# Keys and values of every fourth sequence of a cross attention projected during the feed-forward layer before it

## The reference

```python
x = x + _L0_ffn_ref(_layernorm(x, axis=-1), L0_ffn_w_gate, L0_ffn_w_up, L0_ffn_w_down)
x = x + _L1_xattn_ref(_layernorm(x, axis=-1), ctx_1024, ctx_1024, L1_xattn_Wq, ..., L1_xattn_bo)

def _L1_xattn_ref(x1, x2, Wq, bq, Wk, bk, Wv, bv, Wo, bo):
    q = x1 @ Wq.T + bq ; k = x2 @ Wk.T + bk ; v = x2 @ Wv.T + bv
    ...   # 16 heads
    attn = softmax(q k^T / 4) ; o = attn v
    return o @ Wo.T + bo
```

## Time and profile before

| | us |
|---|---|
| median of 3 runs | 1636.23 |
| lowest, highest | 1634.57, 1638.24 |
| the profiled execution: time | 1634.2 |
| its span | 1632.4 |

### The profile page before, as it was taken

One profiled execution on the slowest core, in us unless ns is written; L12 is line 12 of the kernel. 1 busy time (PEld: TensorE's weight loads), 2 busy tenths in 40 slices (PEclk: granted clock), 3 DMA queues, 4 the chain that ended last, 5 costly groups with the idle time before them and its releaser, 6 DMA issues.

```text
span 1632.4 us, 32837 instructions
## 1 busy us (share of the span) xinstructions
PE 1463.9 (90%) x12556; PEld 1127.3 (69%) x12556; DVE 897.7 (55%) x1896; ACT 712.2 (44%) x1761; POOL 498.9 (31%) x693
## 2 busy tenths in 40 slices
PE   3998996991799999999996688789999999999999
PEld 3887774431677777777775466548877885886787
DVE  3898897488545555565655588734224323422332
ACT  3887775395535554555553455421212211221221
POOL 1445551001026865865553577500000000000000
PEclk9999999995999999999998799989999999999999
DMA  7000000000031161145110000013321440342230
GB/s 280 24 10 2 1 0 1 1 0 27 14 130 40 39 237 46 39 142 211 39 32 2 1 2 0 1 45 136 135 104 50 153 159 13 136 163 76 91 136 13
DMA packets 49500, 111.38 MB, mean 68 GB/s; under 512 B 4240, under 2 KB 6800, under 8 KB 46864
## 3 DMA queue, kind: packets, MB, share of 16 engines
q1 hardware_dynamic: 49424, 110.36, 19.3%
HBM read 99.86 MB, written 10.49 MB: 68 GB/s over the span
## 4 chain that ended last, share of the span: by engine, by line
PE 70%; DVE 15%; issue 6%; POOL 5%; ACT 2%; DMA 1%; SPq 0%; DVEq 0%; POOLq 0%; ACTq 0%
PE ps L843 22%; PE ps L491 15%; PE ps L695 6%; PE ps L497 6%; PE ps L689 5%; PE ps L894 3%; PE ps L715 3%; DVE R L1223 2%; PE ps L667 2%; DVE R L1519 2%; PE ps L726 2%; DVE amax L1392 2%; POOL R L1792 1%; POOL R L1810 1%; PE ps L560 1%
## 5 line engine op out<-in xcount | busy, mean ns | idle before, releaser
L843 PE MATMUL ps<-R 128*128 128x256 f32 x1792 | 388.6, 379 | 3.4 <-DVE R L1649 3.4
L843 PEld LDWEIGHTS ps<-R 128*128 128x128 f32 x1792 | 340.0, 190 | 52.2 <-issue 6.5
L491 PE MATMUL ps<-R 128*128 128x128 f32 (+1 forms) x1344 | 307.3, 388 | 6.4 <-DVE R L1388 4.8
L491 PEld LDWEIGHTS ps<-R 128*128 128x128 f32 x1344 | 190.5, 194 | 119.3 <-issue 109.6
L1792 POOL TENSOR_TENSOR R<-R,c_inv 128x1024 f32<-128x1024 f32 x64 | 121.1, 1893 | 170.4 <-DVE c_inv L1558 170.4
L1109 ACT ACTIVATE R<-ps,c_nmx 128x257 f32<-128x257 f32 x256 | 118.0, 474 | 112.0 <-DVE c_nmx L1543 112.0
L1519 DVE COPY R<-ps 128x512 f32<-128x512 f32 x128 | 88.2, 689 | 106.3 <-PE ps L715 105.1
L689 PE MATMUL ps<-R,x_wk 128*128 128x256 f32 x512 | 128.6, 394 | 0.8 <-POOL R L1784 0.8
L695 PE MATMUL ps<-x_wv,R 128*128 128x256 f32 x512 | 121.1, 379 | 0.0
L1870 POOL TENSOR_SCALAR g_ve<-g_mv 128x4 f32<-128x4 f32 x4 | 0.9, 236 | 345.6 <-DVE g_mv L1611 345.6
L689 PEld LDWEIGHTS ps<-R,x_wk 128*128 128x128 f32 x512 | 92.7, 191 | 17.9 <-POOL R L1784 1.4
(11 more groups left out here) (205 smaller groups left out, 2463.4 us busy)
## 6 DMA issues: line engine op xcount, KB each, us to landing
R<-quadrant_sums SPq DMA_DIRECT2D x32, 1024.0 KB, 6.8
R<-in_f_hq SPq DMA_DIRECT2D x32, 768.0 KB, 4.6
R<-in_ctxT SPq DMA_DIRECT2D x64, 257.0 KB, 2.7
R<-in_f_hq SPq DMA_DIRECT2D x8, 1024.0 KB, 8.3
quadrant_sums<-R SPq DMA_DIRECT2D x8, 1024.0 KB, 7.6
R<-in_f_w SPq DMA_DIRECT2D x3, 1024.0 KB, 7.1
R<-in_ctxk SPq DMA_DIRECT2D x16, 128.0 KB, 2.1
out<-x SPq DMA_DIRECT2D x4, 512.0 KB, 2.6
```

The source lines that it names most:

```text
L491: r = mm(dst, w[:, ki, fo * P:(fo + 1) * P], src[:, ki, :], start=(ki == 0), stop=(ki == KI - 1))
L843: r = mm(ps[:, 4 * (g % 2) + bk, half * HALF:(half + 1) * HALF], f_wr[g % 3][:, w, ki * P:(ki + 1) * P], src[:, k, ki, :], start=(ki == 0) ...
```

## The change

Of each tile, the fourth sequence (u = 3) is projected earlier. Its 16 contexts ("ahead" 0 to 15) are loaded raw (without the last position) into three buffers; PE projects keys and values of them, where the subtraction of the last position is made otherwise: for keys it goes into the bias of ACT's copy (`kb_ahead`), for values a third matmul per half adds minus the last position's value to every row (`nvl_ahead`), so that `values_ahead` has six matmuls where `c_values` has four. ACT copies them out (`stage_ahead`) and SP stores them to a DRAM tensor `kv_ahead`. Ten of the sixteen lie on PE between the gate products and the down products; the other six lie between and behind the four down blocks (10, 11 and 12 behind the first three, 13 to 15 behind the last). In the loop the fourth sequence's keys and values are loaded back from `kv_ahead` (`load_keys`, `load_values`), so POOL's shift, PE's keys and values and ACT's copies are made for three of four sequences. `c_kT` has four buffers, one for each u.

The loop's steps are then: u = 0 as before (keys and values of this tile's third sequence). u = 1: scores, outputs, transposes of both halves of the probabilities, the second into bank 5 rather than 6, then keys of the next tile's first sequence, then `c_project_out`; no values. u = 2: scores, outputs, `c_turn`, first half of the values, transposes, second half of the values, transposes; no keys. u = 3: keys and values of the next tile's second sequence, in the old order. On DVE, at u = 1 the two copies come ahead of the extraction, and `c_add` and `last_stat` move behind the reciprocal. On POOL the shift ahead of step u = 0 is now that of the next tile's first sequence, for which SP can issue the transfer of tile 0 only when the last of the 16 stores has landed (the waits for `ahead_stored` stand in front of SP's loop). On ACT two, not three, up conversions precede the first gate conversion. Some semaphores are merged, and the small tile `w_int` lies in R.

```diff
+        AHEAD, AHEAD_PAUSE = T, 10
+
+        def ahead_no(j):
+            return j + 1 if j < AHEAD_PAUSE else j + 3
+
+        def ahead_bank(j):
+            return 2 * ((j + 1) % 4) if j < AHEAD_PAUSE else 4
+
+        def first_no(u):
+            return AHEAD_PAUSE + u + 1
+
+        def rest_no(m):
+            return AHEAD + m + 1
...
+            def load_ahead(j):
+
+                sp.dma_start(a_ctx[j % 3], A["ctxT"][SPT * j + 3, :, :, 0:S - 1]).then_inc(ctxk_in[j % 3], 16)
+
+            def store_ahead(j):
+
+                sp.wait_ge(k_copied, ahead_no(j))
+                sp.dma_start(kv_ahead[j, :, 0:2, :], a_kT[j % 3]).then_inc(ahead_stored[j % 3], 16)
+                sp.wait_ge(v_copied, ahead_no(j))
+                sp.dma_start(kv_ahead[j, :, 2:4, :].rearrange("p a b -> p (a b)"), a_v[j % 3])\
+                    .then_inc(ahead_stored[j % 3], 16)
...
+            def load_keys(i):
+
+                after(sp, c_s, 2 * SPT * i)
+                sp.dma_start(c_kT[3][:, :, 0:S - 1], kv_ahead[i, :, 0:2, :]).then_inc(k_loaded, 16)
+
+            def load_values(i):
+
+                after(sp, c_o, SPT * i)
+                sp.dma_start(c_v[3], kv_ahead[i, :, 2:4, :]).then_inc(v_loaded, 16)
...
+            for j in range(AHEAD):
+                if j + 3 < AHEAD:
+                    sp.wait_ge(v_ready, ahead_no(j))
+                    load_ahead(j + 3)
+                if j == 3:
+                    sp.wait_ge(f0_gj, 2)
+                    for n in range(3):
+                        sp.dma_start(c_ctx[n], A["ctxT"][n]).then_inc(ctx_in[n], 16)
+                if j >= 1:
+                    store_ahead(j - 1)
+                if j == 5:
+                    sp.wait_ge(ahead_stored[0], 32)
+                    load_keys(0)
+                    load_values(0)
+            store_ahead(AHEAD - 1)
+            for j in range(3):
+                sp.wait_ge(ahead_stored[j], 32 * ((AHEAD + 2 - j) // 3))
...
-                    sp.wait_ge(v_ready, n + 1)
-                    sp.dma_start(c_ctx[u], A["ctxT"][n + SPT]).then_inc(ctx_in[u], 16)
+                    if u < 3:
+                        sp.wait_ge(v_ready, rest_no(3 * i + u) if i or u == 2 else first_no(u))
+                        sp.dma_start(c_ctx[u], A["ctxT"][n + SPT]).then_inc(ctx_in[u], 16)
+                    if u == 1 and i:
+                        load_keys(i)
+                    if u == 3 and i:
+                        load_values(i)
...
-            def c_turn_probs(n, par, k):
-
-                after(pe, c_ptc, 2 * n + k)
+            def c_turn_probs(n, par, k, bank=6):
+
+                after(pe, c_ptc, 2 * n + (k if bank == 6 else 0))
                 for g in (2 * k, 2 * k + 1):
                     for c in range(2):
                         at = ((g % 2) * 2 + c) * P
-                        r = tr(ps[:, 6, at:at + P], c_p[par][:, g, c * P:(c + 1) * P], ident[:])
+                        r = tr(ps[:, bank, at:at + P], c_p[par][:, g, c * P:(c + 1) * P], ident[:])
                 r.then_inc(c_pt, 1)
...
-                pe.wait_ge(k_copied, n + 1)
+                if u == 3:
+                    pe.wait_ge(k_loaded, 16 * (i + 1))
+                else:
+                    pe.wait_ge(k_copied, rest_no(3 * i + u))
...
-                    c_outputs(n - 2, (u + 2) % SPT)
-                more = not (last and u >= 2)
+                    c_outputs(i if u >= 2 else i - 1, (u + 2) % SPT)
                 behind = not (first and u == 0)
-                if more:
-                    pe.wait_ge(ctx_shifted, n + 3)
-                    pe.wait_ge(k_copied, n + 2)
-                    c_keys((u + 2) % SPT)
-                after(pe, c_otc, n - 1)
-                if u == 1 and not first:
-                    c_project_out(i - 1)
-                if u == 2 and not last:
-                    c_turn(i + 1)
-                if u == 3 and not last:
-                    c_query(i + 1)
-                if behind:
-                    pe.wait_ge(c_nrm, n)
-                    c_turn_probs(n - 1, (u + 1) % 2, 0)
-                if more:
-                    pe.wait_ge(v_copied, n + 2)
+                done = 3 * i + 2 if u == 0 else 3 * i + 3 if u < 3 else 3 * i + 4
+
+                def keys():
+                    if u and last:
+                        return
+                    pe.wait_ge(ctx_shifted, done + 1)
+                    pe.wait_ge(k_copied, rest_no(done - 1))
+                    c_keys((2, 0, 0, 1)[u])
+
+                def probs(k, bank=6):
+                    if behind:
+                        pe.wait_ge(c_nrm, n)
+                        c_turn_probs(n - 1, (u + 1) % 2, k, bank)
+
+                def values(c):
+                    if u and last:
+                        return
+                    pe.wait_ge(v_copied, rest_no(done - 1))
+                    c_values((u + 2) % SPT, c)
+
+                if u == 1:
+                    probs(0)
+                    pe.wait_ge(v_copied, rest_no(3 * i + 2))
+                    probs(1, 5)
+                    keys()
+                    if not first:
+                        pe.wait_ge(c_otc, n - 1)
+                        c_project_out(i - 1)
+                elif u == 2:
+                    after(pe, c_otc, n - 1)
+                    if not last:
+                        c_turn(i + 1)
+                    values(0)
+                    probs(0)
+                    values(1)
+                    probs(1)
...
+            def keys_ahead(j, k):
+                pe.wait_ge(ctxk_in[j % 3], 16 * (NT + j // 3 + 1))
+                for fo in range(KI):
+                    for ki in range(KI):
+                        r = mm(ps[:, k, fo * D:(fo + 1) * D], x1_wk[:, ki, fo * P:(fo + 1) * P], a_ctx[j % 3][:, ki, :],
+                               start=(ki == 0), stop=(ki == KI - 1))
+                r.then_inc(k_ready, 1)
+
+            def values_ahead(j, k):
+                for c in range(2):
+                    for ki in range(KI):
+                        mm(ps[:, k, c * D:(c + 1) * D], a_ctx[j % 3][:, ki, c * P:(c + 1) * P], x1_wv[:, ki, :],
+                           start=(ki == 0), stop=False)
+                    r = mm(ps[:, k, c * D:(c + 1) * D], ident[0:AHEAD, j:j + 1].broadcast_to([AHEAD, P]), nvl_ahead[:, :],
+                           start=False, stop=True)
+                r.then_inc(v_ready, 1)
...
+            pe.wait_ge(f0_ugc, 2 * NF0 * NB - 6)
+            for fo in range(KI):
+                for ki in range(KI):
+                    mm(ps[:, 0, fo * AHEAD:(fo + 1) * AHEAD], x1_wk[:, ki, fo * P:(fo + 1) * P], last_ahead[:, ki, 3, :],
+                       start=(ki == 0), stop=(ki == KI - 1))
+            for ki in range(KI):
+                r = mm(ps[0:AHEAD, 1, 0:D], last_ahead[:, ki, 3, :], x1_wv[:, ki, :], start=(ki == 0), stop=(ki == KI - 1))
+            r.then_inc(c_vl_ps, 1)
+
+            for j in range(AHEAD_PAUSE):
+                if j < 3:
+                    pe.wait_ge(f0_ugc, 2 * NF0 * NB - 4 + 2 * j)
+                else:
+                    pe.wait_ge(c_vl_done, 1)
+                    if j > 3:
+                        pe.wait_ge(v_copied, ahead_no(j - 4))
+                keys_ahead(j, ahead_bank(j))
+                if j == 0:
+                    pe.wait_ge(c_vl_done, 1)
+                values_ahead(j, ahead_bank(j) + 1)
...
+            pe.wait_ge(v_copied, ahead_no(AHEAD_PAUSE - 1))
             f0_down(0)
+            ahead(10)
             f0_down(1)
+            ahead(11)
             c_turn(0)
             f0_down(2)
+            ahead(12)
             c_query(0)
             f0_down(3)
+            for j in range(13, AHEAD):
+                ahead(j)
...
+            def stage_ahead(j):
+
+                if j == 2:
+                    act.wait_ge(f0_g2, NF0)
+                if j >= 3:
+                    act.wait_ge(ahead_stored[j % 3], 32 * (j // 3))
+                k = ahead_bank(j)
+                if j == 0:
+                    act.wait_ge(c_vl_done, 1)
+                act.wait_ge(k_ready, ahead_no(j))
+                for fo in range(KI):
+                    r = af(a_kT[j % 3][:, fo, :], ps[:, k, fo * D:(fo + 1) * D], ACT.Identity,
+                           bias=kb_ahead[:, fo, j:j + 1])
+                r.then_inc(k_copied, 1)
+                act.wait_ge(v_ready, ahead_no(j))
+                af(a_v[j % 3], ps[:, k + 1, :], ACT.Copy).then_inc(v_copied, 1)
...
+            act.wait_ge(c_vl_ps, 1)
+            for fo in range(KI):
+                af(kb_ahead[:, fo, :], ps[:, 0, fo * AHEAD:(fo + 1) * AHEAD], ACT.Identity, scale=-1.0,
+                   bias=colb[:, BK1, fo:fo + 1])
+            af(nvl_ahead[:, :], ps[0:AHEAD, 1, 0:D], ACT.Copy, scale=-1.0).then_inc(c_vl_done, 1)
+            for j in range(2):
+                stage_ahead(j)
...
             act.wait_ge(f0_scale, 4)
-            for f in range(NF0):
-
-                after(act, f0_o, f - 3)
```

(37 more changed lines are left out.)

170 lines of the change are left out of this document (94 added, 76 removed).

## The result

| | us |
|---|---|
| before, median of 4 runs | 1636.3 |
| changed, median of 4 runs (lowest, highest) | 1685.39 (1681.83, 1686.41) |
| ratio, 95% interval | 1.0296 [1.0277, 1.0315] |
| profiled execution of the changed kernel: time, span | 1685.78, 1683.9 |

The changed kernel is 3% slower. The prediction had the direction, but 1649 with a range up to 1662: it missed 36 us.

The account below looks back on a forecast made before the run. PE was taken to bound the loop, with idle time only in the feed-forward tail. 23.6 + 2.3 - 14.6 + 3.0 - 1.5 = +12.8 us gave 1647.0 profiled, 1649 on the median, range 1628 to 1662.

Parts of the forecast that it names:

- Prices on PE, the ahead sequence: Keys and values of one ahead sequence on PE, 20 instructions: 4.32 us, taken from between 3.57 and 4.32.
- The feed-forward tail, first down block: Ten ahead sequences overfill PE's 38.6 us idle stretch; first down block starts at 420.3 rather than 419.34, +1.0 us.
- From there to the loop: Four down blocks, query and turn, six uncovered ahead sequences: 68.5 us instead of 45.96; loop starts at 488.9, +23.6.
- First tile: POOL's shift waits for the last ahead store and a load, so PE waits in step 1: +2.3 us.
- A tile: Loop tile 25.57 us against 26.61, with new PE waits of 1.5 in step 1, 1.1 in step 2; tiles 1 to 14: -14.6.
- Rival (d), the clock: Small PE gaps in the loop lower the granted clock, 2.2 us a tile, total 1680; chance 0.06.
- Quadrant tiles: Tiles 3, 4, 8 and 9: quadrant sum and shift delay POOL's multiplication of step 0 by 0.75; +3.0 us together.
- The last tile and what follows: Last tile loses step 1's keys and values but waits, its step 2 reciprocal comes sooner: -1.5 us; what follows untouched.
- Rival (a), the gain: Loop stays bound by PE's work with no new wait: tile 23.04, -50.0 us, about 1614; chance 0.13 in full.

Follow-up runs that it names:

- plain_third: Changed kernel with the third matmul of the ahead values reading the identity's first 128 columns instead of one column read 128 times; 1684.13 us, ratio 1.0289.
- full_third: Changed kernel with the third matmul of the ahead values over all 128 rows, 112 of them zero, instead of 16; 1665.36 us, ratio 1.0185.
- no_third: Changed kernel without the third matmul of each half of the ahead values, so the last position isn't subtracted; 1665.65 us, ratio 1.0163.
- later_loop: full_third with 14 unread matmuls just ahead of the loop, to start it later; 1663.97 us, ratio 1.0185 to the kernel before.
- part9: Changed kernel with only nine sequences ahead, all in the pause; their tiles in the order of reordered, the others in the old order; 1613.5 us, ratio 0.9858.
- part9_full: part9 with the third matmul of full_third, over 128 rows; 1611.26 us, ratio 0.9843 to the kernel before.
- fill: Changed kernel with unread matmuls in the loop's two new PE waits, three in step 1 and two in step 2; 1664.41 us, ratio 1.0168.
- keys_first: Changed kernel with the keys moved ahead of the transposes in step 1 on PE; 1667.91 us, ratio 1.0187.
- reordered: keys_first, plus DVE's extraction ahead of the copies in step 1 and half of the values ahead of `c_turn` in step 2; 1629.75 us, ratio 0.9958.

## Why the prediction came out too low

The profiled time was 1685.8 where the sum gave 1647.0, 38.7 us more. By the prediction's own steps:

- **Prices on PE, the ahead sequence: 4.32, measured 5.10.** The step named the unknown, bounded it from 3.57 to 4.32, and took the price of the keys and values in the earlier trace rows as the upper end. The upper end was no end: the change of the stationary operand's rows makes these instructions and the next ones later than an instruction of either kind, 0.31 for 0.22 us. plain_third and full_third show it. It reaches the time twice, over ten sequences in the pause and six in the tail (0.78 each).
- **The feed-forward tail, first down block: 420.3, measured 429.46.** 2.9 of the 9.2 are the gate products' later start in this execution, 6.3 are the price of the ten. That ten of 4.32 just fit was right, as full_third shows; only the size was off.
- **From there to the loop: 68.5, measured 74.7.** Six times 0.78 are 4.7. (Four blocks at 10.4 are 41.6, not 41.4, which would have made it 68.7.) The other 1.5 to 1.9 are the first down block: I took its slow clock as lost with the idle stretch, but there is a wait of 2.07 us in front of it, for DVE's first block of the input, and behind it the clock fell once more (12.1 us for 48 instructions, 10.4 for the later ones; in no_third it did not fall). Against the instants described under later_loop, waits of 2.06 to 2.08 us here begin at 0.26 to 1.39 in the nine kernels where the clock fell, and at 1.77 to 2.67 in the three where it did not (no_third, part9, part9_full). The wait had been in the earlier trace rows as a part of the 7.47.
- **First tile: +2.3, measured +4.3.** The chain was right, and each of its members near: the last store was issued 0.7 behind the loop's start, the context transfer 2.7, POOL's shift began 5.5 and its multiplication 6.5 behind it (7.5 worked out), PE waited 3.48. The store and the load thus took 2.0 and 2.8 us, 4.8 in a row, and the trace agrees with the at least 4 that the prediction took from the Trainium skill (DMA: Bandwidth & Descriptors, Anatomy of one DMA), though that section is about transfers issued by GpSimd and these were SP's. What made it longer is the clock once more: 9.49 for step 1 here, in later_loop 4.21 with a wait of 0.77.
- **A tile: 25.57, measured 25.88 with the clock kept** (plain tiles of fill and full_third; 25.97 and 25.80 in the changed kernel's tiles 1 and 14). Steps 1 and 2 came out at 6.73 and 5.84 for 6.50 and 5.70. The method (each engine's chain from the start of the scores) gave both waits within 0.1 us, and no rival for the waits was needed. This is 4.3 over 14 tiles.
- **Rival (d), the clock, at 0.06.** This is where the sum failed in the loop: ten of the tiles 1 to 14 lost 1.2 to 1.5 us each, 14.8 in all. I weighed it down by one row of another stage (34.55 us of work in 40 at 1.00). That row has nearly the same share of work as the changed tile (22.49 in 25.90, 0.87), so a share does not tell the two apart; where the waits lie counts, as the traces read under later_loop show. The Trainium skill (TensorE: Matmul & The Clock Gate, A second HAM failure mode: psum-queue depth-cycling) reports of one kernel that short idle times between groups of matmuls made the clock fall again and again. In most tiles of the changed kernel it did so, behind a wait of 1.40 us; in ten tiles of full_third, behind the same wait, it did not, nor behind that of 1.6 in keys_first. The page names the danger; the prediction set it aside by a row that could not tell.
- **Quadrant tiles: +3.0, measured 0.65 each (26.53 for 25.88), 2.6.** Right.
- **The last tile and what follows: -1.5, measured +1.2.** The last tile's step 1 took 7.59 (6.65 in fill, where the clock was kept): with no keys in it a second wait of 1.62, for the extraction, follows the first, and the clock fell in its course.

The parts of the miss: 2.9 and 6.3 ahead of the down block, 6.2 in the tail, 2.0 in tile 0, 18.7 in tiles 1 to 14 (14.8 of the clock and 3.9 of the steps), 2.7 at the end. Two causes, the third matmul (6.3 and 4.7) and the clock (14.8, 1.5 to 1.9 in the first down block, up to 2.0 in the first tile), are three quarters of it. Why the clock fell behind the wait in ten of fourteen tiles of the changed kernel, of no_third and of plain_third, but in four of full_third's and three of later_loop's, is **shown only as far as the traces go**: where the wait lay against the instants at which the clock can change separates all 70 waits, and nothing else that differs is needed for it. It is read from one execution of each kernel, and no experiment was made on it.

Rival (a), the gain, was held back by the two waits as argued, but reordered shows how little held it: two calls moved on PE and one on DVE.

## What to carry to other kernels

When work is taken out of a loop that is bound by one engine, list what that work had covered, for each wait in the loop, and move something else into that place in the same change; here that turned +3.0% into -0.4%. Work moved into an idle stretch is worth its price only as far as the stretch goes: count the pieces that fit (nine of 4.32 us here, with the tenth at break-even), and leave the others where they are, which gave 1.4 to 1.6%. And where waits of more than a microsecond come into a dense run of matmuls, carry the loss of the clock as a case with a real chance: here it cost 14.8 us in the tiles, against 36.5 us of the two waits (22.2 and 14.3).

## What the runs showed of the hardware

- fp32 matmuls of 256 columns whose stationary operand has 16 rows, set between those of 128 rows, took 0.31 us per instruction by starts, and the next group started late too; with 128 rows, 112 of them on zeros, 0.22. Filling up the rows made a sequence of 20 instructions 0.78 us shorter, from 5.10 to 4.32.
- An idle time of PE of 1.40 us, in a tile with 87% of PE work, made the granted clock of the tile fall to 0.94 in most tiles of one kernel and left it at 1.00 in most of another with the same loop. In tile 2 the clock was 0.50 from 566.3 to 569.6 and 1.00 on both sides. In five kernels the place of the wait against the instants at which the recorded clock changes separates the falls from the others, 70 waits of 70. Where it fell, the eight key instructions behind it took 2.76 us instead of 1.8. Behind a wait of 2.07 us the first down block took 12.1 us by starts in the changed kernel and 10.4 in no_third.
- One program's executions spread over 14 us (1660.1 to 1674.7), in step with the mean granted clock.
